# A mixture of experts computed block by block for the chosen tokens, in place of every expert for every token

## What is computed

```
scores = sigmoid(x @ gate_w)                       # 32 per token
top 2 of 4 groups of experts by their best score; in them the top 6 experts
weights = chosen scores / their sum
g = ragged_dot(xs, w_gate); u = ragged_dot(xs, w_up)          # xs: chosen tokens, sorted by expert
d = ragged_dot(silu(g) * u, w_down)                            # 256 -> 176 -> 256
expert_out = sum over the 6 of d * weight
shared = silu(x @ sw_gate) * (x @ sw_up) @ sw_down             # 256 -> 352 -> 256
x = x + expert_out + shared
```

## Time and profile before

| | |
|---|---|
| median of 3 runs | 5795.54 us (5794.55 to 5802.18) |
| the profiled execution, its own time | 5799.74 us |
| its span, from first to last instruction | 5798.0 us |
| TensorE busy / weight load | 5087.0 us (88%) / 3946.4 us (68%) |
| VectorE, ScalarE, GpSimd busy | 4113.1 us (71%), 2942.4 us (51%), 1769.9 us (31%) |
| mean granted TensorE clock | 0.937 |
| DMA | 335.94 MB in 236073 packets, 58 GB/s over the span |

### The profile page before, as it was taken

How to read it: one execution, slowest core, us unless ns; L and a number is a source line. 1 busy time by engine, 2 the same in 40 slices (tenths; PEclk the granted TensorE clock), 3 DMA queues, 4 the chain that set the end, 5 groups by cost and what they waited for, 6 DMA issues and landing times. The chain is left out here.

```text
span 5798.0 us, 123840 instructions
## 1 busy us (share of the span) xinstructions
PE 5087.0 (88%) x42624; PEld 3946.4 (68%) x42624; DVE 4113.1 (71%) x7679; ACT 2942.4 (51%) x5385; POOL 1769.9 (31%) x2002
## 2 busy tenths in 40 slices
PE   6589999999999999999977999996788888888865
PEld 3367777777777777777766666664566676766754
DVE  7667777777777777777755555556677777777767
ACT  3245555555555555555542333332466666666643
POOL 4454444444444444444401333332000000000003
PEclk8799999999999999999988999997899999999976
DMA  2311221122122212211122000000333333333320
GB/s 76 98 50 43 51 57 44 47 51 51 41 51 56 51 40 51 57 48 43 41 76 82 25 24 24 24 24 19 99 94 88 86 86 86 88 95 86 86 55 24
DMA packets 236073, 335.94 MB, mean 58 GB/s; under 512 B 85202, under 2 KB 199762, under 8 KB 225343
## 3 DMA queue, kind: packets, MB, share of 16 engines
q1 hardware_dynamic: 235598, 329.13, 21.9%
HBM read 169.46 MB, written 85.85 MB: 44 GB/s over the span
## 5 line engine op out<-in xcount | busy, mean ns | idle before, releaser
L684 POOL TENSOR_TENSOR a_ksq<-a_kb 125x512 f32<-125x512 f32 x384 | 399.1, 1039 | 705.1 <-DVE a_kb L634 703.7
L1621 DVE TENSOR_SCALAR_CACHE_REDUCE b_pr<-b_ps 112x1500 f32<-112x1500 f32 x256 | 439.4, 1716 | 245.5 <-PE b_ps L1696 245.5
L599 ACT ACTIVATE a_pTh<-a_pt 125x448 f16<-125x448 f32 x768 | 402.7, 543 | 325.4 <-PE a_pt L758 320.8
L656 DVE CUSTOM_DVE_ANT_0 a_pr<-a_ps,a_mask 112x1500 f32<-112x1500 f32 x256 | 439.8, 1718 | 165.0 <-PE a_ps L105 162.8
L103 PE MATMUL a_po<-a_vh,a_pTh 125*112 125x128 f16 x3072 | 549.3, 219 | 3.7 <-DVE a_pTl L672 3.1
L105 PE MATMUL a_po<-a_vh,a_pTl 125*112 125x128 f16 x3072 | 547.3, 219 | 0.0
L104 PE MATMUL a_po<-a_vl,a_pTh 125*112 125x128 f16 x3072 | 546.9, 219 | 0.0
L1578 ACT ACTIVATE b_pTh<-b_pt 125x448 f16<-125x448 f32 x768 | 392.7, 542 | 302.8 <-PE b_pt L1709 298.7
L1628 DVE TENSOR_TENSOR b_pTl<-b_pt,b_pTh 125x448 f16<-125x448 f32 x768 | 454.0, 616 | 71.9 <-ACT b_pTh L1578 68.7
L1709 PE MATMUL b_pt<-ident,b_pr 112*125 112x112 f32 x3072 | 474.0, 294 | 32.2 <-DVE b_pTl L1628 27.0
L672 DVE TENSOR_TENSOR a_pTl<-a_pt,a_pTh 125x448 f16<-125x448 f32 x768 | 464.8, 619 | 30.9 <-ACT a_pTh L599 25.3
(11 more groups left out here) (336 smaller groups left out, 14926.1 us busy)
## 6 DMA issues: line engine op xcount, KB each, us to landing
b_ks<-b_kn SPq DMA_DIRECT2D x384, 187.5 KB, 4.5
scratch_cT<-a_cT SPq DMA_DIRECT2D x128, 375.0 KB, 3.1
b_cT<-scratch_cT SPq DMA_DIRECT2D x32, 1500.0 KB, 6.7
a_ctx<-ctx SPq DMA_DIRECT2D x32, 1440.0 KB
scratch_o<-a_ot SPq DMA_DIRECT2D x64, 224.0 KB
m_ot<-scratch_o SPq DMA_DIRECT2D x16, 896.0 KB, 5.5
scratch_qh<-q_qTh SPq DMA_DIRECT2D x32, 224.0 KB, 2.3
scratch_ql<-q_qTl SPq DMA_DIRECT2D x32, 224.0 KB, 2.4
```

The lines of the kernel that those rows point to most:

```text
L599: nc.scalar.activation(pTh[:, r % 2, 4 * third:4 * third + 4].rearrange("p k c -> p (k c)"), ps_t[n % 2][0:KP, 0:4 * RP], ACT.Copy).then_i ...
L656: nc.vector.tensor_tensor_reduce(out=pr[:, n % 2].rearrange("p (a k) -> p a k", k=500), in0=ps_s[0:RP, :, 0:500], in1=mask[:].rearrange("p ...
L684: nc.gpsimd.tensor_tensor(ksq[:, kt % 2], kb[0:KP, kt % 4], kb[0:KP, kt % 4], ALU.mult).then_inc(s["k_squared"], 1)
L1621: nc.vector.tensor_scalar(pr[:, n % 2].rearrange("p (a k) -> p a k", k=500), ps_s[0:RP, :, 0:500], -1.0, None, ALU.mult, ALU.min, accum_ou ...
```

## The change

Each token's row of 256 numbers is copied to a place of a table `scratch_xd` in DRAM for each expert it chose, sorted by expert and padded to blocks of 128 rows. There are 18432 rows in 144 blocks: 116 for the routed experts (`NBX`, the most that 6 times 1792 tokens can need, whatever the routing), and twice 14 for the two halves of the shared expert. All 144 are always computed. Step by step:

- `q0_phase` fills the 116 routed blocks with zeros, by 4 DMAs on ScalarE's queue, and ScalarE waits for them at the phase's end.
- `mix0_phase` no longer keeps `g.xT`. GpSimd writes each tile's rows as high and low halves (`rows`), and SyncE stores them twice to the shared blocks and the residual to `scratch_xs` (`keep`, in SyncE's order behind `load_o` and `load_x`). Behind the last tile, VectorE and TensorE work out the row (slot) of each token for each chosen expert and the expert of each block (`g.be`).
- A new `dispatch_phase` clears `g.wg`, loads and splits the weights of all 34 experts into SBUF (`g.wg`, `g.wd`, 50048 and 34816 float16 per partition), and GpSimd scatters rows by 96 indirect DMAs of 112 rows.
- `blocks_phase` replaces `experts_phase`: 72 steps (`NS`) of 2 blocks (`SB`). SyncE loads 256 rows of `scratch_xd` with a transposing DMA, TensorE reads the two blocks' experts from `g.be` with `value_load` before `up` and again before `down`, and addresses the weights by that number. `up` is 36 matmuls of 128 columns, `down` 10 of 256. The rows of the result are stored to `scratch_yd`.
- `q1_phase` fetches, for each tile, the token's 6 rows of `scratch_yd` by 6 indirect DMAs on GpSimd and its 2 shared rows by 2 DMAs on SyncE, and VectorE adds the 8 to the residual (`gather`), which SyncE loads once from `scratch_xs`.

The program's text grows by 183 lines. Its core:

```diff
@@ q0_phase, ScalarE
+            act.wait_ge(zeroed, 1)
+            for n in range(4):
+                part = io.xd[n * NBX // 4 * BT:(n + 1) * NBX // 4 * BT, :].rearrange("(b p) d -> p b d", p=BT)
+                act.dma_start(part, zero[:].unsqueeze(1).to_broadcast([BT, NBX // 4, 2 * H])).then_inc(empty, 16)
...
@@ mix0_phase, SyncE
+            def keep(t, k, _):
+                sp.wait_ge(s["rows"], 2 * t + 2)
+                for n in range(2):
+                    sp.dma_start(io.xd[ds(t * TT + (NBX + NBS * n) * BT, TT), :],
+                                 xr[:, k].rearrange("p n d -> p (n d)")).then_inc(kept[k], 16)
+                sp.dma_start(io.xs[ds(t * TT, TT), :], ...
+            pipeline(sp, NT, [(load_o, 2), (load_x, 1), (keep, -1)])
...
@@ mix0_phase, VectorE and TensorE, behind the last tile
+            nc.vector.tensor_copy(sel[:], er[:, :, 0:NE]).then_inc(s["picked"], 1)
...
+            for t in range(NT):
+                last = nc.tensor.matmul(pN[0:NE, 0:128], sel[:, t], ones[0:TT, :], start=(t == 0), stop=(t == NT - 1))
...
+            for t in range(NT):
+                own(nc.vector.max(s8[:, t], g.slot[:, t]))
...
@@ dispatch_phase
+            for t in range(NT):
+                pool.wait_ge(x_in[t % XR], 16 * (t // XR) + 16)
+                for k in range(TOPK):
+                    nc.gpsimd.indirect_dma_start(io.xd, bass.IndirectOffsetOnAxis(g.idx[:, t, k:k + 1], 0),
+                                                 xr[:, t % XR], None).then_inc(sent[t % XR], 16)
...
+                nc.scalar.activation(main(e, 0), stg[:, par, :, :, 0:128], ACT.Copy, scale=WS).then_inc(s["w_hi"], 1)
+                for u in range(2):
+                    nc.scalar.activation(tail(e, 0, u), stg[:, par, :, u, 128:M], ACT.Copy,
+                                         scale=WS).then_inc(s["w_hi"], 1)
+                nc.scalar.activation(g.wd[:, e, 0], std[:, par], ACT.Copy, scale=WS).then_inc(s["w_hi"], 1)
...
+            nc.vector.memset(g.wg[:], 0.0).then_inc(s["cleared"], 1)
...
@@ blocks_phase
+                wait(sp, s["up_done"], t - 1)
+                sp.dma_start_transpose(out=xb[:, k].rearrange("p n c q -> p (n c) q"),
+                                       in_=io.xd[ds(t * TC, TC), :]).then_inc(x_in[k], 16)
...
+            def expert(t, b):
+                return pe.value_load(g.be[0:1, ds(SB * t + b, 1)], min_val=0, max_val=NX - 1)
+            def up(t, k, half):
+                held = [expert(t, b) for b in range(SB)]
+                pe.wait_ge(x_in[k], 16 * half + 16)
+                wait(pe, s["h_ready"], 2 * (t - 1))
+                for b in range(SB):
+                    e, cols = held[b], slice(b * BT, (b + 1) * BT)
+                    for n in range(3):
+                        m = slice(128 * n, min(128 * n + 128, WG))
+                        for c in range(KC):
+                            last = three_products(nc, ps[k][n][0:m.stop - m.start, cols], g.wg[:, ds(e, 1), 0, c, m],
+                                                  g.wg[:, ds(e, 1), 1, c, m], xb[:, k, 0, c, cols], xb[:, k, 1, c, cols],
+                                                  start=(c == 0), stop=(c == KC - 1))
...
+            pipeline(pe, NS, [(up, 0), (down, -1)])
...
@@ q1_phase
+            def fetch(t, k):
+                wait(pool, s["whole"], t - 1)
+                for n in range(TOPK):
+                    nc.gpsimd.indirect_dma_start(yk[:, k, n], None, io.yd,
+                                                 bass.IndirectOffsetOnAxis(g.idx[:, t, n:n + 1], 0)).then_inc(y_in[k], 16)
...
+            for t in range(NT + 2):
+                if t < NT:
+                    fetch(t, t % 2)
+                if t >= 2:
+                    rstd(t - 2, t % 2, 0)
...
+                for n in range(2):
+                    q(nc.vector.scalar_tensor_tensor(xrow, ysh[:, k, n], 1 / WS, xrow, ALU.mult, ALU.add)).done()
...
+                for n in range(TOPK):
+                    w = g.wk[:, ds(t, 1), n:n + 1].rearrange("p a n -> p (a n)")
+                    ins = nc.vector.scalar_tensor_tensor(xrow, yk[:, k, n], w, xrow, ALU.mult, ALU.add)
```

More of the change, by code:

```diff
@@ new lines, in _ @@
+            dve.wait_ge(s["counted"], 1)
+            passed(dve, gate)
+            own(nc.vector.tensor_scalar(need[:], pN[0:NE, 0:128], 1.0 / BT, 0.5 - 0.5 / BT, ALU.mult, ALU.add)).done()
+            nc.vector.tensor_scalar(need16[:], need[:], MAGIC, MAGIC, ALU.add, ALU.subtract).then_inc(s["padded"], 1)
+            dve.wait_ge(s["placed"], 1)
+            passed(dve, gate)
+            starts = pX[0:TT, 0:NE].unsqueeze(1).to_broadcast([TT, NT, NE])
+            own(nc.vector.tensor_copy(slot[:], pL[0:TT, :].rearrange("p (t e) -> p t e", e=NE))).done()
@@ L1073, in load, with rows @@
                 sp.dma_start(std[0:MT, par, 1, :], srcs[2][128:M]).then_inc(w_in[par], 16)
-            load(0, 0)
-            load(1, 1)
-            with sp.Fori(0, (NE - 2) // 2) as i:
-                for k in range(2):
-                    sp.wait_ge(s["w_lo"], 5 * (2 * i + k) + 5)
-                    load(2 * i + k + 2, k)
-            for n in range(2):
-                sp.wait_ge(s["w_lo"], 5 * (NE - 2 + n) + 5)
-                load(0, n, shared=n)
+            def rows(t):
+                wait(sp, sent[t % XR], 16 * TOPK * (t // XR))
+                sp.dma_start(xr[:, t % XR], io.xd[NBX * BT + t * TT:NBX * BT + (t + 1) * TT, :])\
+                    .then_inc(x_in[t % XR], 16)
@@ new lines, in _ @@
+            for t in range(XR):
+                rows(t)
+            for e in range(NX):
+                wait(sp, s["w_lo"], 4 * (e - 1))
+                if e < NE:
+                    load(e, e % 2)
+                else:
+                    load(0, e % 2, shared=e - NE)
+                if e % 2 and XR + e // 2 < NT:
+                    rows(XR + e // 2)
+        @block.gpsimd
+        def _(pool):
+            for t in range(NT):
[3 more added lines that the diff above has]
+                                                 xr[:, t % XR], None).then_inc(sent[t % XR], 16)
+            for n in range(XR):
+                pool.wait_ge(sent[n], 16 * TOPK * (NT // XR))
@@ L1104, in _, with low @@
-            each(pool, NX, step)
-        def main(t, par, c, n):
-            return t[:, par, n, c, 0:256].rearrange("p (u m) -> p u m", m=128)
-        def tail(t, par, c, n):
-            return t[:, par, n, c, 256:384].rearrange("p (u m) -> p u m", m=64)[:, :, 0:MT]
+            def low(t, k, _):
+                pool.wait_ge(s["h_hi"], t + 1)
+                wait(pool, s["h_lo"], 2 * t)
+                passed(pool, gate)
+                nc.gpsimd.tensor_tensor(hl[:, k], hb[:, k, 0], hh[:, k, 0], ALU.subtract).then_inc(s["h_lo"], 1)
+                pool.wait_ge(s["h_lo"], 2 * t + 1)
+                passed(pool, gate)
+                nc.gpsimd.tensor_tensor(hh[0:MT, k, 1], hb[64:64 + MT, k, 1], hh[64:64 + MT, k, 1],
+                                        ALU.subtract).then_inc(s["h_lo"], 1)
@@ L1112, in _ @@
+            pipeline(pool, NS, [(low, 0)])
         @block.scalar
         def _(act):
[L1114 to L1123 removed]
@@ L1197, in _, with take @@
+            def take(t, k, half):
+                dve.wait_ge(s["down_done"], t + 1)
+                wait(dve, y_out[k], 16 * half)
+                nc.vector.tensor_copy(yb[:, k], pd[k][:]).then_inc(s["y_ready"], 1)
+            pipeline(dve, NS, [(product, 0), (take, -1)])
         @block.tensor
         def _(pe):
[L1199 to L1213 removed]
@@ L1235, in _ @@
-            steps(pe, step)
-            down(NX - 1, (NX - 1) % 2, NC4 - 1)
+            def expert(t, b):
[12 more added lines that the diff above has]
+                                                  start=(c == 0), stop=(c == KC - 1))
+                last.then_inc(s["up_done"], 1)
@@ new lines, in down @@
+            def down(t, k, _):
+                held = [expert(t, b) for b in range(SB)]
+                pe.wait_ge(s["h_lo"], 2 * t + 2)
+                wait(pe, s["y_ready"], t - 1)
+                for b in range(SB):
+                    e, cols, out = held[b], slice(b * BT, (b + 1) * BT), pd[k][:, b]
+                    three_products(nc, out, hh[:, k, 0, cols], hl[:, k, cols], g.wd[:, ds(e, 1), 0, 0],
+                                   g.wd[:, ds(e, 1), 1, 0], start=True, stop=False)
+                    for n in range(2):
+                        last = nc.tensor.matmul(out, hh[0:64 + MT, k, 1, cols], g.wd[0:64 + MT, ds(e, 1), n, 1],
+                                                start=False, stop=(n == 1))
+                last.then_inc(s["down_done"], 1)
@@ L1272, in _, with load @@
             sp.dma_start(bq[:], io.bq1.rearrange("(a n) -> a n", a=1).to_broadcast([TT, H])).then_inc(b_in, 16)
+            def load(t, k, _):
+                wait(sp, s["whole"], t - 1)
+                for n in range(2):
```

(2 more changed lines are left out.)

392 lines of the change are left out of this document (224 added, 168 removed).

## The result

| | before | changed |
|---|---|---|
| median of 14 runs | 5795.1 us | 5824.6 us |
| changed to before | | 1.0050, 95% interval 1.0039 to 1.0061 |
| the profiled execution's span | 5798.0 us | 5816.2 us |

The account below looks back on a forecast made before the run. The experts stage was taken as bound by TensorE. Terms 10 + 5 + 11 - 843 + 165 + 422 + 71 = -159 gave 5640.7 from 5799.7 us, 5637 against the median; own range 5570 to 5700, whole range 5490 to 5840.

Parts of the forecast that it names:

- the blocks term: `blocks_phase`: 72 steps of 5.7 us (`up` 2.6, `down` 1.1, reads 2.0) plus 12 for start and end, +422 us.
- The table read: TensorE's sequencer in the blocks stage: 0.39 us per read, bounds 0.04 and 0.59; four with register instructions 2.0 a step.
- Rival A: Blocks stage: TensorE's sequencer does register work and reads while the array works; step 4.1 us, whole 5522 us; chance 0.17.
- Rival B: Blocks stage: TensorE's clock falls to half; step about 7.2 us, 108 us more, whole 5745 us; chance 0.14.
- Rival C: Dispatch and layer 1's queries: indirect DMAs dear on GpSimd, at 2.3 us each +180, whole 5817 us; chance 0.12.
- Rival D: Blocks stage: the transposing load lands late; step 8.6 us, 209 us more, whole 5846 us; chance 0.12.
- Stores in `mix0_phase`: Loop of `mix0_phase`: `keep` ahead of later loads, mostly hidden by two tiles' lead; +5 us, bounds 0 and 30.
- Zeroing: `q0_phase`: 15.2 MB of zeros, only first loads sharing the DMA engines exposed; +10 us, bounds 0 and 55.
- Routing tail: Behind the `mix0_phase` loop: more passes, maxima, small matmuls and handovers between engines; +11 us, bounds 8 and 20.
- Dispatch: New stage: clearing 21.8 us, then 96 indirect DMAs at 1.36 us and about 10 of ends; +165 us, bounds 157 and 250.
- Queries of layer 1: `q1_phase`: 16 tiles at 8.7 us plus 17 for fetching ahead and the end, 156 us for 85; +71 us.
- GpSimd decides: Layer 1's queries: GpSimd's six indirect DMAs and power, 8.7 us a tile, set the time over VectorE's 8.1.

Follow-up runs that it names:

- the three with cheaper reads: Changed kernel with two of a step's four table reads left out, two numbers per read, or four per read: blocks stage 457.9, 528.4, 493.0 us for 555.4.
- The three mends: Changed kernel with zeroing in 16 parts, row stores a tile later, only unused weight columns cleared: first stage 239.1 us, dispatch 169.8 us.

## Why the prediction was wrong

- **The step that failed** is the blocks term: "a step is s = 2.6 + 1.1 + 2.0 = 5.7 us". It is 7.55, or 7.65 with the longer ones of every second step: `up` 3.0 for 2.6, because a register instruction costs the sequencer 0.125 us from one to the next, not the 0.05 of its own duration; the reads 3.0 for 2.0, because a read is paid with its value's way through register, check and register; and 0.5 of loop and waits that the sum didn't have. The stage is 555.4 for 422, and these 133 us are most of the 177 between forecast and the profiled execution. That TensorE's own instruction stream was the bound was said, and the experiments bear it out; its price was taken at the durations of single rows, and the gaps between sequencer instructions were left out.
- **The table read** was taken at 0.39 from SyncE's issue. The row of the read itself is 0.30, below that; with the 0.15 until the register has it some 0.5, and as a whole step 0.68 to 0.75. The floor of 600 ns that the Trainium skill states ("DMA: Bandwidth & Descriptors", section "Latency and other measured facts") lies nearer to the whole, and its 6.5 us a step nearer to the result than 5.7. The trace disagrees with it for the bare read: 0.294 us at the least, 0.300 in the median of 288.
- **Rival A**, that the sequencer runs ahead, is false as it was meant: without the reads and registers the step falls to 3.7, so their work had not been hidden. The sequencer does run ahead, but it is itself what takes longest. **Rival B**, half clock: the clock did fall, to 0.78 on average, but the array was done before the sequencer in both steps shown, and the steps of the changed kernel and of the three with cheaper reads follow the sequencer's sum. **Rival C**, indirect DMAs: 1.24 us from one to the next against 1.36 taken; the longest of the 192 took 1.63 beside a busy VectorE (0.94 in the median), so the standstill that this rival reckoned with isn't seen here. **Rival D**: the load issues in 1.24 us and lands in 3.2, and hides. The kernel came out slower by none of the four, but by a sum that was too low in four places: blocks, stores, zeroing and queries.
- **Stores in `mix0_phase`**: +5 forecast, +41.6 measured, beyond the bound of 30. The order on SyncE's queue was named, and then the lead of two tiles was trusted; but the lead is spent when the load's own turn comes behind a wait for the tile that is not yet done.
- **Zeroing**: +10 for +27.9, within the bounds, by another way than said: not the first loads sharing the DMA engines (`q_wst` landed in 8.3 us), but ScalarE held for 36 us by its own issues.
- **Routing tail** (+11, measured +9.4) was right. **Dispatch** (165, measured 167.9) was right in its number by luck. The forecast had the scatters decide behind the clearing, 131 + 10 + 21.8. The memset is 20.9, but the first scatter comes only at 29.6, the scatters take 125 to their last start, and the stage ends with the weights, for which it had 3.6 us an expert and which took 4.0.
- **Queries of layer 1**: +71 for +86.2. The step "GpSimd decides" failed: with half the fetches the stage is only 3 us shorter. GpSimd and VectorE are both near full there, with 8.0 and 8.3 us of work in 9.6, and GpSimd's first fetch of a tile waits 1.5 us for VectorE's last addition; the forecast had 8.7, the larger of the two and nothing for the handover.
- **Attention of layer 1**: 31 us that the forecast had at nothing. 25 of them go when the loop is moved, so they come mostly from its place in the program: luck, without which the result would have been further off. Moved away, the changed kernel is 0.85% slower than before.

The three mends, blocks of 256 and a good place for the loop make the idea pay: 5556.0 us, 4.1% faster than before.

## What to carry to other kernels

A number read at run time is paid on the engine that uses it: here 0.125 us for each address that is computed and 0.7 for each number read, against matmuls of 0.055 at the high clock. Count them per unit of work and make the unit large, before counting the work saved. A store that waits for its data must not stand ahead of a load in one queue, and a bulk DMA of megabytes must be cut up or its issuing engine be idle. And compare kernels by stage: the whole hides a stage that moved by 10 to 25 us because its loop came to lie elsewhere.

## What was not expected of the hardware

- The code of a hardware loop of some 1780 instructions on TensorE was loaded again in each turn (9 loads of 16 KB, 138 in the stage) or hardly at all (38), and moving the loop by 64 to 100 instructions changed which. Within one execution a turn with loads took 94.8 to 95.2 us, one without 89.4 to 91.9.
- Single register instructions of 46 ns stand 0.125 us apart on TensorE's sequencer, with one matmul between them or two.
- Four DMAs of 3.8 MB held the issuing engine for 36.45 us, with the DMA engines full, and DMAs of 1184 KB out of 74 partitions moved at 48 GB/s and held it for 16.5 us each in the median.
- A transposing DMA of 256 rows of 1 KB took 1.24 us to issue and 3.2 to land; the plain load of 187.5 KB takes 4.5.
